# Attention inside a one-core transformer chain: a new table of order, one weighing block per group of heads, the input norm one sample ahead, and two alternating buffers

## The chip, the cores and the metric

The kernel runs on one NeuronCore of a Trainium2 chip. The metric is the device time of one execution in microseconds (us), as the median of several runs; lower is better.

## The reference

Four layers in a row on `x` of 8 samples x 512 tokens x 256 features. The change touches only the attention half of the first layer:

```python
x = _ln(src) * (1.0 + scale) + shift                 # norm of the input, modulated per sample
q = (x @ Wq + bq).reshape(B, S, N_HEAD, HEAD_DIM)    # 16 heads of 16; k and v likewise
scores = jnp.einsum('bhqd,bhkd->bhqk', q / math.sqrt(HEAD_DIM), k) + attention_bias
scores = jnp.where(src_mask, -jnp.inf, scores)
probs = jax.nn.softmax(scores, axis=-1)
ctx = jnp.einsum('bhqk,bhkd->bhqd', probs, v)        # merged to [B, S, D]
x = x + (ctx @ Wo + bo)                              # the residual is the scaled x, not src
```

Then follow a feed-forward part, an adapter layer, a pairwise rotation and a second adapter layer. `attention_bias` is 8 x 16 x 512 x 512 float32, 128 MiB, which is read once.

## The kernel before, in words

The attention part handles the samples b = 0 to 7 one after the other. A sample has 64 **steps** n, one for each head h = n // 4 and tile t = n % 4 of 128 queries. Each engine runs its own program over the steps, and semaphores join them. In step n:

- PE makes scores three steps ahead (`scores`, L581): 128 queries x 512 keys into one of three banks `s_bank`. For some tiles it adds the mask term by a second matmul (L583).
- DVE adds the bias two steps ahead and takes the row maximum (`add_bias`, L762), into one of four tiles `prob`.
- ACT takes the exponential in place (L937).
- PE transposes the 128 x 512 tile in four pieces (`turn`, L593) into one of two banks `t_bank`; ACT (L944) or DVE (L771, for the steps in `DVE_TAKES`) copies it to `pt`.
- After four heads, PE multiplies `pt` with the values for the whole group (`weigh(b, g, c)`, L607) for the four key blocks c. One float32 matmul stands as two records in the trace.

The mask is 0 or -1e30. For the tiles counted in `POOL_TILES[h]`, POOL adds it to the loaded bias in place (`mask_bias`, L1101, up to four tiles in one instruction), and the other tiles are the PE ones. The bias of one head is a load of 1 MiB into one of four buffers `big`; SP issues the load for head h + 4 when the last tile of head h has been read by `add_bias`.

Between the steps stand **spare uses** of two further banks, at the steps that the tables `TAIL`, `AHEAD`, `VALUES` and `GROUPS` give: `XT` transposes the normed x of the next sample, `Q`, `K`, `V` project it, `O` transposes a group's context, `C` and `W` are the output projection of the previous sample. POOL cuts the projections into three bf16 pieces (`cut`), SP stores the pieces to DRAM and loads them back stacked (`stack_q`, `stack_k`).

The norm of the next sample's x is made inside the same sample in which it is used: DVE takes the statistics at step 11, ACT takes the square root at step 12 (L949), DVE inverts it and norms four tiles at step 14 (`normalise`, L801), and PE transposes them at steps 14 and 15 (L629). The scaled result goes to `xt`. POOL copies it to `xres` (`keep_residual`, L1172), because `W` of that sample comes a whole sample later. POOL makes the mask term twice for each sample, once for heads 0 to 13 and once for heads 14 and 15 (L1078, L1087).

PE, ACT, POOL and SP run samples 1 to 6 in a hardware loop; DVE has its program written out.

## Time and profile before

| What | Value |
|---|---|
| Median of 3 runs | 1039.73 us (1037.82 to 1042.37) |
| Span of the profiled execution, first to last instruction | 1036.6 us |
| PE matmul busy | 956.1 us, 92% |
| DVE, ACT, POOL busy | 813.7, 734.7, 726.3 us |
| One of the six steady samples (290.70 to 374.66) | 83.96 us |
| Start and setup, up to the first `add_bias` | 39.8 us |
| All after 710 us (the end of attention, and the network part) | 326.6 us |

The profiled execution is described by its span; its own device time is not listed apart from it, and the median of the runs lies 3.1 us above the span. The busy shares are over the whole run. A steady sample is measured from the first `add_bias` of one sample to that of the next, so that its length is what a sample costs.

### The profile page before, as it was taken

What the parts mean: (1) busy time and instruction counts of PE and PEld (TensorE: products, weight loads), DVE (VectorE), ACT (ScalarE), POOL (GpSimd) and SP (SyncE); (2) the same over time, 40 slices, a digit from 0 to 9 for tenths busy, and PEclk for the clock granted to TensorE, in tenths of its full rate; (3) what the DMA queues carried; (4) which work ended last, traced back from release to release, by engine and by line L of the source; (5) the groups of instructions that cost most, each with busy time, mean ns of one, the idle gap of its engine ahead of it and who ended that gap; (6) DMA issues with size and microseconds to landing.
All of it is one profiled execution on the core that took longest, in us unless ns stands there. A gap on an engine that the chain in (4) does not pass through costs nothing. (4 is left out here: it accounts for less than half of the span.)

```text
span 1036.6 us, 20438 instructions
## 1 busy us (share of the span) xinstructions
PE 956.1 (92%) x5892; PEld 640.9 (62%) x5892; DVE 813.7 (78%) x2075; ACT 734.7 (71%) x1211; POOL 726.3 (70%) x596
## 2 busy tenths in 40 slices
PE   5879999999999999999999999898999999999963
PEld 4646556656655655755665665454777777777752
DVE  8887797878879879879787887874456877887697
ACT  3577887888798788788788878875446556655433
POOL 3487697788788878878778878777555567755631
PEclk9989999999999999999999999999999999999987
DMA  7978978997996997897799799752111111111001
GB/s 262 334 289 292 381 289 278 363 347 238 346 384 214 336 386 257 291 390 292 265 372 343 237 348 370 252 193 82 41 41 41 42 33 50 42 41 41 21 21 41
DMA packets 127535, 230.33 MB, mean 222 GB/s; under 512 B 5488, under 2 KB 53872, under 8 KB 123632
## 3 DMA queue, kind: packets, MB, share of 16 engines
q1 hardware_dynamic: 127472, 229.60, 62.0%
q8 instruction: 26, 0.43, 0.2%
q14 instruction: 37, 0.30, 0.1%
HBM read 187.63 MB, written 41.94 MB: 221 GB/s over the span
## 5 line engine op out<-in xcount | busy, mean ns | idle before, releaser
L937 ACT ACTIVATE prob<-prob,nmax 128x512 f32<-128x512 f32 x512 | 357.0, 729 | 59.6 <-DVE nmax L762 56.4
L762 DVE CUSTOM_DVE_ANT_0 prob<-s_bank,big 128x512 f32<-128x512 f32 x512 | 338.7, 684 | 69.7 <-POOL big L1101 40.3
L1101 POOL TENSOR_TENSOR big<-big,mterm_early 128x2048 f32<-128x2048 f32 (+2 forms) x88 | 305.3, 3484 | 71.5 <-DMA big<-in_fside_Bx16xSxS 62.3
L593 PEld LDWEIGHTS t_bank<-ident,prob 128*128 128x128 f32 x2048 | 238.1, 141 | 168.3 <-issue 51.5
L593 PE MATMUL t_bank<-ident,prob 128*128 128x128 f32 x2048 | 317.7, 278 | 15.9 <-ACT prob L937 6.7
L944 ACT COPY pt<-t_bank 128x512 f32<-128x512 f32 x312 | 181.1, 584 | 51.7 <-PE t_bank L593 50.6
L581 PE MATMUL s_bank<-stack_k,stack_q 128*128 128x512 bf16 x512 | 195.4, 382 | 1.3 <-DVE nmax L762 0.7
L771 DVE COPY pt<-t_bank 128x512 f32<-128x512 f32 x200 | 137.2, 686 | 34.9 <-PE t_bank L593 34.6
L2052 POOL TENSOR_TENSOR gl<-big,gh 128x512 fp32r<-128x512 f32 x64 | 84.6, 1329 | 69.8 <-DVE gh L1643 69.8
L607 PE MATMUL o_bank<-pt,val 128*32 128x512 f32 x1024 | 122.9, 598 | 1.2 <-ACT pt L944 0.7
L1905 ACT ACTIVATE big<-bank,late 128x512 f32<-128x512 f32 x62 | 42.7, 689 | 75.2 <-PE bank L1446 71.4
L1101 POOL TENSOR_TENSOR big<-big,mterm_late 128x1024 f32<-128x1024 f32 (+1 forms) x16 | 49.9, 3119 | 29.2 <-DMA big<-in_fside_Bx16xSxS 29.2
L581 PEld LDWEIGHTS s_bank<-stack_k,stack_q 128*128 128x128 bf16 x512 | 50.0, 98 | 25.4 <-DVE nmax L762 12.0
L607 PEld LDWEIGHTS o_bank<-pt,val 128*32 128x32 f32 x1024 | 26.9, 109 | 59.4 <-issue 55.7
L583 PE MATMUL s_bank<-mterm_early,ident_bf 128*128 128x512 bf16 x152 | 57.9, 381 | 0.0
L637 PE MATMUL spare<-xth,w_parts 128*128 128x512 f32 x128 | 52.6, 428 | 1.7 <-DVE xtl L809 1.7
L1464 PE MATMUL bank<-gh,w2h 128*128 128x512 f32 x128 | 53.5, 418 | 0.0
L1446 PE MATMUL bank<-xth,w1h 128*128 128x512 f32 x124 | 50.6, 408 | 1.0 <-PEq L291 1.0
L1464 PE MATMUL bank<-gh,w2l 128*128 128x512 f32 x128 | 50.5, 395 | 0.0
L1446 PE MATMUL bank<-xtl,w1h 128*128 128x512 f32 x124 | 49.0, 395 | 0.0
L1446 PE MATMUL bank<-xth,w1l 128*128 128x512 f32 x124 | 48.9, 395 | 0.0
L762 DVE DVE_READ_ACCUMULATOR2_ANT nmax<- 128x1 f32 x512 | 42.1, 82 | 0.0
(257 smaller groups left out, 1610.0 us busy)
## 6 DMA issues: line engine op xcount, KB each, us to landing
big<-in_fside_Bx16xSxS SPq DMA_DIRECT2D x128, 1024.0 KB, 8.0
pieces_dram<-pieces SPq DMA_DIRECT2D x64, 384.0 KB, 7.3
stack_q<-pieces_dram SPq DMA_DIRECT2D x15, 1024.0 KB, 8.3
stack_k<-pieces_dram SPq DMA_DIRECT2D x15, 1024.0 KB, 10.0
pieces_dram<-pieces SPq DMA_DIRECT2D x32, 256.0 KB, 7.6
xin<-in_x SPq DMA_DIRECT2D x8, 512.0 KB, 8.7
x_dram<-x SPq DMA_DIRECT2D x8, 512.0 KB, 2.6
x1r<-x_dram SPq DMA_DIRECT2D x8, 512.0 KB, 4.3
```

The costliest lines, as they stand in the source:

```text
L581: last = pe.matmul(bank, stack_q[:, h, t * P:(t + 1) * P], stack_k[:, h, :], start=True, stop=not by_pe)
L583: last = pe.matmul(bank, ident_bf[:], mterm[:, t, :], start=False, stop=True)
L593: last = pe.transpose(t_bank[n % 2][:, c * P:(c + 1) * P], prob[:, n % NT, c * P:(c + 1) * P], ident[:])
L607: last = pe.matmul(o_bank[VW * j:VW * (j + 1), :], val[:, c, G * g + j, :], pt[:, pt_slot(G * g + j), c, :], start=(c == 0), stop=(c == QT ...
L762: dve.tensor_tensor_reduce(out=prob[:, n % NT, :], in0=s_bank[n % 3][:, :], in1=bias[:, h % NB, t, :], scale=-1.0, scalar=3e38, op0=ALU.ad ...
L771: dve.tensor_copy(pt[:, pt_slot(h), :, t * P:(t + 1) * P], t_bank[n % 2][:, :].rearrange("p (c q) -> p c q", c=QT)).then_inc(evac[1].sem, 1)
L937: act.activation(tile, tile, ACT.Exp, bias=nmax[:, n % NT:n % NT + 1], scale=-1.0).then_inc(exped.sem, 1)
L944: act.copy(pt[:, pt_slot(h), :, t * P:(t + 1) * P], t_bank[n % 2][:, :].rearrange("p (c q) -> p c q", c=QT)).then_inc(evac[0].sem, 1)
L1101: pool.tensor_tensor(bias[:, h % NB, tiles], bias[:, h % NB, tiles], mterm[:, tiles], ALU.add).then_inc(masked.sem, 1)
L1446: last = pe.matmul(bank[f % 2][:, :], w[:, c, col], h[:, c, :], start=(n == 0), stop=(n == len(parts) - 1))
L1464: last = pe.matmul(bank[c][:, :], w[:, f, c * P:(c + 1) * P], gx[:, f, :], start=(m == 0), stop=(m == len(parts) - 1))
L2052: pool.tensor_tensor(gl[:, f], g[:, f % NGT], gh[:, f], ALU.subtract).then_inc(gl_done.sem, 1)
```

## The change

It does six things.

1. **One weighing block.** `weigh` for the four key blocks of a group stood as two blocks of two, two steps apart. Now all four stand together, at steps 18, 34, 50 and 2.
2. **The norm a sample ahead.** Statistics of the x of sample b + 1 are taken during sample b (steps 21, 26, 47, 48), aggregated at 49, and its four tiles are normed one by one at steps 57, 61, 62 and 63. The inverse root is a power of -0.5 on POOL (step 52), not a root on ACT. The load of x moves from the start of a sample to head 4 of the sample before. In the first sample, which has nobody ahead of it, this is squeezed into steps 3 to 11.
3. **Two buffers for the scaled x**, by parity of the sample; `xres` and `keep_residual` go.
4. **Two buffers for the mask term**, by parity; it is made once for each sample, and two PE waits become one.
5. **The table of order** is another: 46 instead of 43 tiles of a sample masked by POOL, 26 instead of 25 copies by DVE, all spare uses at other steps, and POOL's masks among its other work in another order.
6. **Written-out programs** for PE, ACT and POOL in place of their loops.

The core of the diff:

```diff
-POOL_TILES = (0, 4, 2, 4, 3, 4, 4, 2, 4, 4, 0, 0, 2, 4, 2, 4)
+POOL_TILES = (0, 4, 0, 4, 4, 4, 4, 4, 4, 4, 4, 3, 0, 4, 3, 0)
-HEADS_OF_LOADS = dict(x1=3, first=2, expert=4, W1=6, mask=5, store_0=7, store_1=11)
+HEADS_OF_LOADS = dict(x=4, x1=3, first=2, expert=4, W1=6, mask=5, store_0=6, store_1=13)
-TAIL = [("O", 3, 6, 1), ("C", 0, 7, 1), ("C", 1, 9, 1), ("W", 0, 10, 1), ("W", 1, 12, 1)]
+TAIL = [("O", 3, 4, 1), ("C", 0, 6, 1), ("C", 1, 8, 1), ("W", 0, 10, 1), ("W", 1, 13, 1)]
...
                     g, c = (n - WEIGH_AFTER) // 16, (n - WEIGH_AFTER) % 16
-                    if c in (0, 2) and (g >= 0 or not first):
-                        for part in (c, c + 1):
+                    if c == 0 and (g >= 0 or not first):
+                        for part in range(QT):
                             weigh(b if g >= 0 else b - 1, g % NG, part)
...
+            def normalise_tile(b, t):
+                if t == 0:
+                    dve.wait_ge(root_done.sem, root_done.at(b, 1))
+                done = dve.tensor_scalar(xin[:, t], xin[:, t], mv[:, t, 0:1], rstd[:, t:t + 1], ALU.subtract, ALU.mult)
+                if t == QT - 1:
+                    done.then_inc(xhat_done.sem, 1)
...
-                    dve.wait_ge(res_done.sem, res_done.at(b - back - 1, 1))
                     dve.wait_ge(x1_out.sem, x1_out.at(b - back, 0))
-                    dve.scalar_tensor_tensor(x1[:, i], s[:, :], vec["bo"][:, i:i + 1], xres[:, i],
+                    dve.scalar_tensor_tensor(x1[:, i], s[:, :], vec["bo"][:, i:i + 1], xts[(b - back) % 2][:, i],
                                              ALU.add, ALU.add).then_inc(x1_done.sem, 1)
...
+                    if ahead and n in STATISTICS_AT:
+                        statistics_of(b + 1, STATISTICS_AT.index(n))
+                    if ahead and n == AGGREGATE_AT:
+                        aggregate(b + 1)
+                    if ahead and n in NORMALISE_AT:
+                        normalise_tile(b + 1, NORMALISE_AT.index(n))
...
+            def inverse_root(b):
+                pool.wait_ge(shifted.sem, shifted.at(b, 1))
+                apart(pool, k["apart"])
+                pool.tensor_tensor(rstd[:], std[:], minus_half[:], ALU.pow).then_inc(root_done.sem, 1)
```

`statistics_of(b, t)` takes one tile; the one for t = 0 waits for the load of x. On SP, `load_x(b + 1)` waits until both halves of sample b's scaled x are made.

Three places show how instructions move. The first is PE around the first group's weighing in the first sample: scores (`s_bank`), transposes of a step (`t_bank`), and weighing (`o_bank`). Before:

```order
L581 MATMUL s_bank<-stack_k,stack_q 128x512
L607 MATMUL o_bank<-pt,val 32x512 x8
L593 MATMUL t_bank<-ident,prob 128x128 x4
L581 MATMUL s_bank<-stack_k,stack_q 128x512
L593 MATMUL t_bank<-ident,prob 128x128 x4
L581 MATMUL s_bank<-stack_k,stack_q 128x512
L607 MATMUL o_bank<-pt,val 32x512 x8
L593 MATMUL t_bank<-ident,prob 128x128 x4
```

And of the change:

```order
L622 MATMUL spare<-ident,xin 128x128 x4
L574 MATMUL s_bank<-stack_k,stack_q 128x512
L600 MATMUL o_bank<-pt,val 32x512 x16
L586 MATMUL t_bank<-ident,prob 128x128 x4
L574 MATMUL s_bank<-stack_k,stack_q 128x512
L586 MATMUL t_bank<-ident,prob 128x128 x4
```

The sixteen matmuls stand in one piece, and the second half of the transposed x stands right before them.

The second place is DVE behind the scaled x. In the change, the first statistics of the next sample (`stats<-xin`) come this soon after the second half of the scaled x (`xt_odd<-spare`), on which the load of `xin` waits:

```order
L833 TENSOR_SCALAR xt_odd<-spare,ada 128x512
L816 TENSOR_TENSOR xtl<-xt_odd,xth 128x512 x2
L755 ISA prob,nmax<-s_bank,big 128x512
L755 ISA nmax 128x1
L755 ISA prob,nmax<-s_bank,big 128x512
L755 ISA nmax 128x1
L764 COPY pt<-t_bank 128x4x128
L755 ISA prob,nmax<-s_bank,big 128x512
L755 ISA nmax 128x1
L764 COPY pt<-t_bank 128x4x128
L770 BN_STATS stats<-xin 128x6
```

Before, the four statistics stood together at step 11, with the load issued at the start of the sample:

```order
L762 ISA prob,nmax<-s_bank,big 128x512
L762 ISA nmax 128x1
L777 BN_STATS stats<-xin 128x6 x4
L780 BN_AGGR mv<-stats 128x2 x4
L762 ISA prob,nmax<-s_bank,big 128x512
```

So between the freed `xin` and its next use there are now three additions of bias and two copies, where there were eleven steps.

The third place is DVE at the end of a sample, where three of the four normed tiles now stand between the additions of bias:

```order
L755 ISA prob,nmax<-s_bank,big 128x512
L755 ISA nmax 128x1
L800 TENSOR_SCALAR xin<-xin,mv,rstd 128x256
L755 ISA prob,nmax<-s_bank,big 128x512
L755 ISA nmax 128x1
L800 TENSOR_SCALAR xin<-xin,mv,rstd 128x256
L755 ISA prob,nmax<-s_bank,big 128x512
L755 ISA nmax 128x1
L800 TENSOR_SCALAR xin<-xin,mv,rstd 128x256
L842 RECIPROCAL rsum<-spare 128x16
```

Before they stood together, right ahead of the transposes that read them:

```order
L799 RECIPROCAL rstd<-std 128x4
L801 TENSOR_SCALAR xin<-xin,mv,rstd 128x256 x4
L844 SCALAR_TENSOR_TENSOR x<-spare,vecs,xres 128x512
L762 ISA prob,nmax<-s_bank,big 128x512
L762 ISA nmax 128x1
```

They moved from step 14, where PE waits for them, to the last steps of the sample before.

## Rows read from the trace of the kernel before

**Rows 1.** The windows view: one steady sample (290.70 to 374.66), busy us by engine.

```profile
290.70:374.66 83.96, 80.98 (x559) 50.39 (x558) 69.67 (x184) 69.94 (x119) 67.76 (x54) 1.00 0.88 316
```

**Rows 2.** The groups of the whole run: line engine operation, busy, mean ns, idle before.

```profile
L937 ACT ACTIVATE prob<-prob,nmax 128x512 f32<-128x512 f32 x512 | 357.0, 729 | 59.6 <-DVE nmax L762 56.4
L762 DVE CUSTOM_DVE_ANT_0 prob<-s_bank,big 128x512 f32<-128x512 f32 x512 | 338.7, 684 | 69.7 <-POOL big L1101 40.3 <-PE s_bank L581 15.5 <-PE s_bank L583 7.4
...
L944 ACT COPY pt<-t_bank 128x512 f32<-128x512 f32 x312 | 181.1, 584 | 51.7 <-PE t_bank L593 50.6
L771 DVE COPY pt<-t_bank 128x512 f32<-128x512 f32 x200 | 137.2, 686 | 34.9 <-PE t_bank L593 34.6
L607 PE MATMUL o_bank<-pt,val 128*32 128x512 f32 x1024 | 122.9, 598 | 1.2 <-ACT pt L944 0.7 <-issue 0.5
...
L583 PE MATMUL s_bank<-mterm_early,ident_bf 128*128 128x512 bf16 x152 | 57.9, 381 | 0.0
```

**Rows 3.** The timeline of PE at the end of a group of weighing blocks: start, us.

```profile
317.05 0.38 PE L581 MATMUL s_bank<-stack_k,stack_q 128*128 128x512 bf16 x1
317.27 0.38 PE L583 MATMUL s_bank<-mterm_early,ident_bf 128*128 128x512 bf16 x1
317.48 0.60 PE L593 MATMUL t_bank<-ident,prob 128*128 128x128 f32 x4
317.92 0.38 PE L581 MATMUL s_bank<-stack_k,stack_q 128*128 128x512 bf16 x1
318.23 1.92 PE L607 MATMUL o_bank<-pt,val 128*32 128x512 f32 x16
320.08 0.66 PE L593 MATMUL t_bank<-ident,prob 128*128 128x128 f32 x4
```

**Rows 4.** The timeline of PE, 305.5 to 308.5: ahead of the output projection.

```profile
307.24 1.12 PE L662 MATMUL spare<-cont,wo 128*128 128x512 f32 x2 [0.76 <-ACT cont L976]
```

**Rows 5.** The timeline of PE, 312 to 316: ahead of the turned x.

```profile
313.41 0.66 PE L593 MATMUL t_bank<-ident,prob 128*128 128x128 f32 x4 [0.29 <-ACT prob L937]
315.47 0.66 PE L629 MATMUL spare<-ident,xin 128*128 128x128 f32 x4 [1.41 <-DVE xin L801]
```

**Rows 6.** The timeline of ACT in the same stretch.

```profile
309.65 1.28 ACT L949 ACT_TABLE_LOAD   x1
310.95 0.30 ACT L949 ACTIVATE std<-mv,eps 128x4 f32<-128x4 f32 x1
311.26 1.28 ACT L937 ACT_TABLE_LOAD   x1
```

**Rows 7.** The source view of L801, normalise: ns min/median/max.

```profile
L801 DVE TENSOR_SCALAR xin<-xin,mv,rstd x32: 398/774/4156, 13.7 to 566.6; 128x256 f32<-128x256 f32 x32
```

**Rows 8.** The timeline of POOL, one steady sample.

```profile
312.56 2.71 POOL L1087 TENSOR_SCALAR mterm_late<-mraw 128x512 bf16<-128x512 uint8 x4
316.25 1.05 POOL L1172 TENSOR_SCALAR xres<-xt 128x1024 f32<-128x1024 f32 x1 [0.98 <-issue]
...
326.16 4.12 POOL L1101 TENSOR_TENSOR big<-big,mterm_early 128x2048 f32<-128x2048 f32 x1 [2.69 <-DMA big<-in_fside_Bx16xSxS]
...
338.61 4.11 POOL L1101 TENSOR_TENSOR big<-big,mterm_early 128x2048 f32<-128x2048 f32 x1 [0.20 <-POOL pieces L1055]
...
377.44 4.09 POOL L1101 TENSOR_TENSOR big<-big,mterm_early 128x2048 f32<-128x2048 f32 x1 [3.28 <-DMA big<-in_fside_Bx16xSxS]
```

**Rows 9.** The timeline of the SP queue: a load of bias, and the first store of pieces.

```profile
320.39 0.38 SPq L430 DMA_DIRECT2D big<-in_fside_Bx16xSxS  x1
...
335.27 5.58 SPq L457 DMA_DIRECT2D pieces_dram<-pieces  x6
```

**Rows 10.** The DMA view: issues, KB each, us from issue to landing.

```profile
big<-in_fside_Bx16xSxS SPq DMA_DIRECT2D x128, 1024.0 KB, 8.0
...
xin<-in_x SPq DMA_DIRECT2D x8, 512.0 KB, 8.7
```

**Rows 11.** The timeline of PE in the first sample.

```profile
61.30 1.12 PE L629 MATMUL spare<-ident,xin 128*128 128x128 f32 x4 [3.39 <-DVE xin L801]
```

More of the change, by code:

```diff
@@ L268, in parts, with first_use @@
     return 2 if what in "QKVW" else 1
-def firsts(first, h, t):
-    return [t for n in range(QT * first, QT * h) if n % QT == t and t >= POOL_TILES[n // QT]]
+def first_use(h, t):
+    return all(t < tiles for tiles in POOL_TILES[:h])
 class SpareBanks:
@@ L737, in _ @@
             iteration(0, first=True)
-            with pe.Fori(1, B - 1) as b:
+            for b in range(1, B - 1):
                 iteration(b)
@@ L819, in spare_use @@
                 elif what == "XT":
-                    if i == 0 and not first:
-                        dve.wait_ge(res_done.sem, res_done.at(b - 1, 1))
                     if banks.kind == "last":
@@ L855, in iteration @@
                         take_turned(b, n - 1)
-                    if not last and n == STATISTICS_AT:
-                        statistics(b)
-                    if not last and n == NORMALISE_AT:
-                        normalise(b)
+                    if first and n == FIRST_STATISTICS_AT:
+                        for t in range(QT):
+                            statistics_of(b, t)
+                        aggregate(b)
+                    if first and n in FIRST_NORMALISE_AT:
+                        normalise_tile(b, FIRST_NORMALISE_AT.index(n))
+                    if ahead and n in STATISTICS_AT:
[4 more added lines that the diff above has]
+                        normalise_tile(b + 1, NORMALISE_AT.index(n))
                     if last and n == NORMALISE_LAST:
@@ L1026, in _ @@
             iteration(0, first=True)
-            with act.Fori(1, B - 1) as b:
+            for b in range(1, B - 1):
                 iteration(b)
@@ L1177, in iteration @@
                         copy_values(b - 1, NG - 1)
-                    if n == RESIDUAL_AT and not first:
-                        keep_residual(b - 1)
+                    if n == FIRST_ROOT_AT and first:
+                        inverse_root(b)
+                    if n == ROOT_AT and not last and not before_last:
+                        inverse_root(b + 1)
                     if not last and n in CUT_STEPS:
@@ L1207, in _ @@
             iteration(0, first=True)
-            before = links[0]
-            with pool.Fori(1, B - 1) as b:
+            for b in range(1, B - 2):
                 iteration(b)
-            assert links[0] - before == per_link
+            iteration(B - 2, before_last=True)
             iteration(B - 1, last=True)
```

219 lines of the change are left out of this document (99 added, 120 removed).

## The prediction

> **What bounds the kernel now.** I first cut the run into samples with the windows view. The steady ones are alike, so I read one: it takes 83.96 us, and PE is busy for 80.98 of them, DVE for 69.67, ACT for 69.94 and POOL for 67.76; the clock column stands at 1.00, PE's full level [rows 1]. The last column but one is the DMA share, 0.88. So PE ends the waits in the steady part, but no engine has more than 16.2 us to spare, and the DMA engines even less. Whatever shortens PE's chain by much more than 5 us per sample will meet the others.
>
> "Busy" hides how PE's time is made up, so I read starts, not durations. In the timeline a scores matmul is followed by the next instruction after 0.22 us, a mask matmul after 0.21 us, the four transposes of a step after 0.44 us [rows 3]. The 0.38 to 0.66 us of the rows are latencies that overlap. Then I looked for places where one start comes later than that: these are what the change can remove.
>
> **The weighing blocks.** Scores ahead of a weighing block hold PE for 0.31 us in place of 0.22, so going in costs 0.09 us. The block of 16 records takes 1.85 us until the next transposes begin. It is busy for 1.92 us, and one record lasts 0.60 on the mean [rows 2], so the last starts 1.32 us after the first: four rounds of four records at 0.44 us each are 1.76 us, which leaves 0.09 us for going out [rows 3]. That is about 0.2 us for each block. There are eight blocks in a sample and will be four: 0.8 us less. The page "TensorEngine Tiling (Array Packing)" of the Trainium skill says that changing the tiling mode drains the engine; the trace agrees, with the 0.09 us on either side.
>
> Longer blocks (3.7 us) starve the others only if these run out of work. PE is three steps of scores ahead, which is 2.1 us of DVE work (684 ns each) and 2.2 us of ACT work (729 ns each), and copies and spare evictions fill the rest [rows 2]. I cost this at nothing; without that cover it could be 1 us a block on DVE, which has the slack.
>
> **The mask matmuls.** Three fewer in a sample: 3 x 0.21 = 0.63 us less on PE [rows 3]. POOL pays: four tiles take 4.1 us, so three cost 3.1 us; it gets back 2.7 us for the second mask term and 1.05 us for the copy to `xres` [rows 8], and pays for the root of four columns. No row shows that root inside attention; it lies between nothing and a mask instruction of one tile (4.1 / 4 = 1.0 us), and I take the 1.0. POOL's total stays within 0.5 us of what it was (3.1 + 1.0 - 2.7 - 1.05). DVE takes one copy more (0.69 us) and ACT one less (0.58 us) [rows 2].
>
> **The output projection.** `W` stands right behind the second `C`, and waits 0.76 us for ACT's copy [rows 4]. In the new table a step lies between (8 and 10), which is at least 0.66 us of PE work plus its own transposes ahead of `W`. The wait goes: 0.76 us.
>
> **The norm.** ACT switches its table, takes a root of 0.30 us, and switches back: 2.86 us in which no exponential runs [rows 6]. Behind it PE waits 0.29 us for an exponential, and then 1.41 us for the normed tiles [rows 5]. With the norm a sample ahead both waits go: 1.70 us, and ACT has 2.9 us more room.
>
> **What replaces it.** Two new waits can arise, and I price both.
>
> First, x. The load of the next x can go out only when both halves of this sample's scaled x are made, at step 18, and DVE wants its first tile at step 21. A load of x lands 8.7 us after issue [rows 10]. What lies between on PE is one block of 3.7 us and two to four steps of 0.66 us, 5.0 to 6.3 us. So DVE waits 2.4 to 3.7 us in each sample. Behind it on DVE stand the additions of bias for steps 24 and later. PE has scores and exponentials for three steps in hand at that moment, and these steps are long because of the projections in them. Most of the wait is covered; between 0 and 3.7 us reach PE, and I take 0.6, near the covered end.
>
> Second, the port. A normed tile takes between 398 and 4156 ns, with a median of 774 [rows 7]. The 4.1 us are as long as one of POOL's mask instructions, 4.09 to 4.12 us [rows 8]: one instruction of DVE was held for one whole instruction of POOL. So far the tiles stood beside the four short instructions of the mask term (2.71 us together), hence the median. Now the last three stand at steps 61 to 63, while POOL's first mask of the next sample begins when its load lands: at 377.44, which is 2.8 us into the sample, before the change [rows 8]. One tile in each sample may meet it, and be held for between 0 and 4.1 us. PE then has two to three steps in hand again. Between 0 and 4.1 us I take 0.6, because only one of four can meet a given mask instruction and the next steps are PE's long ones.
>
> The rule for this is in "SBUF — State Buffer" of the Trainium skill (section "SBUF: two separate sides"): a VectorE instruction in its fast two-port mode and a GpSimd instruction exclude each other for the whole instruction. The trace agrees, by the 4156 ns.
>
> **The sum for a steady sample**: 0.80 + 0.63 + 0.76 + 1.70 = 3.89 us off, 1.2 us back, 2.7 us net, or 81.3 us in place of 84.0. DMA share becomes 0.88 x 84.0 / 81.3 = 0.91, still below one. Six such samples give 16.2 us.
>
> The first sample waits 3.39 us for its normed tiles alone [rows 11]; its statistics now come at step 3 and its tiles between POOL's first masks, each of which may hold one tile. I take 3 us off, between 0 and 7 (3.39 for the wait, 2.86 for the tables, 0.63 for the mask matmuls). The last sample loses switching, mask matmuls and the wait of `W`, but has no norm ahead: 0.8 + 0.63 + 0.76 = 2.2 us. Start and network part have the same work, apart from copies of nothing that PE waits for. Writing out the loops costs instruction fetches; DVE is written out already and is not short of instructions, so I cost it at zero.
>
> In all 16.2 + 3 + 2.2 = 21.4 us. Against the profiled span that is 1036.6 - 21.4 = 1015.2 us. The median of the runs lies 3.1 us above the span, so I say 1018 us.
>
> **Rivals.**
>
> A, *everything is gained* (0.18): neither new wait reaches PE. Then a steady sample gives 3.9 us, the first one 7, together 23.3 + 7 + 2.2 = 32.5, or 1007 us; ACT's extra room could add up to 1 us per sample, down to 1001. For it: PE's lead of three steps. Against: DVE's share on the last 16 steps, which get both the four tiles and the copies.
>
> B, *slower through the port* (0.13): the four tiles each meet a mask instruction and are held for half of it. That is 4 x 2.05 = 8.2 us per sample on DVE, and near the sample's end nothing covers it. The sample becomes 84.0 - 3.9 + 8.2 = 88.3 us, six of them cost 26 us more, and the time is about 1061 us. It decides from 1 us per tile on PE's path (3.9 / 4). For it: 4156 ns. Against: POOL still waits for its bias load 3.28 us at that point [rows 8], so it cannot be in mask instructions all the time.
>
> C, *given back* (0.12): the wait for x is not covered, 3.5 us of it reach PE, and the port costs 0.6. Then 3.9 - 4.1 is nothing for the steady samples, and the rest saves 2 to 5 us: 1035 to 1038 us.
>
> D, *the change's own POOL table comes late* (0.10). The load for head 11 now stands behind the first store of pieces in the SP queue, whose six issues hold the queue for 5.58 us [rows 9], and they wait for two cuts that POOL makes only behind head 8's mask. Head 11 was free of POOL before and now has three tiles on it. Counting 8.0 us to land [rows 10] after the last issue and 3.1 us of mask, its first tile is ready about when PE wants it, to within 1.5 us. If this and head 14 (now behind the last cut) come late, a sample loses 1.5 us more: 21.4 - 9 = 12.4 off, 1027 us. For it: DVE already waits 40.3 us in the run for POOL's masks [rows 2].
>
> **How the numbers follow.** My forecast (0.47) is 1018 us, with a range of its own of 1010 to 1026. The 80% range must reach A's middle and most of C: 1001 to 1037. Beyond lie B and a little of A. No change, within 0.5% (5.2 us, about what a measurement of this kernel can tell), is 1034.5 to 1045: C and the lower end of B, 0.12. Slower is the rest of B, 0.12. Faster is the forecast, A and D, and the edge of C: 0.76.
>
> **What would show it.** Steady samples of about 81 us; weighing in four blocks of 32 records with only four slow entries and exits; no table load on ACT inside attention; `W` without its wait; the transposes of xin without theirs. On DVE, a wait of the first BN_STATS for a DMA of 2.4 to 3.7 us, and normed tiles of 0.4 us with one of 1 to 4 us at the end of each sample. I am wrong if PE waits for DVE for more than 1.2 us behind those two places, or for POOL's masks of heads 9 to 14, or if DMA landing times rise above 9 us because the same bytes move in less time.

## The result, and the profile after

The changed kernel takes 1059.0 us (1053.2 to 1063.6, 4 runs) beside 1040.4 us for the kernel before: a ratio of 1.017, 95% interval 1.012 to 1.022. I forecast 1018 us. In all ratios below disturbed runs are left out, in the medians they are not, so where the two differ I go by the ratio. The kernel before took 1040.0 to 1041.3 us beside the other runs.

The profiled run of the change has a span of 1051.3 us, 14.7 us more than before. From first addition of bias to the next one, the samples take (us):

| Kernel | sample 0 | samples 1 to 6 | mean of 1 to 6 | sample 7 |
|---|---|---|---|---|
| before | 83.0 | 84.0 83.9 84.0 83.9 83.9 84.1 | 84.0 | 80.1 |
| changed | 90.1 | 85.3 83.3 82.9 86.3 90.4 80.6 | 84.8 | 82.9 |

So 7.1 us come in the first sample, 4.9 in the six steady ones, 2.8 in the last. The steady ones are not alike any more, which is the first thing to see. The windows view of the change, by sample (columns: stretch, us, busy us of PE, PEld, DVE, ACT, POOL, granted clock, DMA share, GB/s), then short stretches in the first and sixth sample:

```profile
38.80:128.80 90.00, 74.61 (x500) 48.99 (x499) 81.60 (x190) 65.04 (x109) 68.19 (x46) 0.92 0.87 309
214.20:297.40 83.20, 77.67 (x537) 49.69 (x538) 71.16 (x186) 66.53 (x113) 65.04 (x49) 0.98 0.89 310
466.60:557.00 90.40, 81.61 (x561) 53.05 (x559) 78.82 (x186) 67.74 (x114) 68.32 (x49) 0.96 0.86 299
...
56.00:60.00 4.00, 0.39 (x1) 0.10 (x1) 4.00 (x4) 0.72 (x1) 4.00 (x2) 0.57 0.51 190
60.00:64.00 4.00, 1.51 (x5) 0.85 (x5) 4.00 (x5) 0.72 (x1) 3.54 (x1) 0.50 0.00 0
64.00:68.00 4.00, 2.96 (x12) 2.47 (x13) 3.54 (x11) 3.08 (x6) 0.00 (x0) 0.50 0.21 66
498.00:502.00 4.00, 0.00 (x0) 0.00 (x0) 4.00 (x2) 0.00 (x0) 3.48 (x1) 0.79 0.59 242
502.00:506.00 4.00, 3.87 (x11) 2.56 (x11) 4.00 (x12) 2.55 (x4) 0.00 (x0) 0.50 0.07 10
```

Beside [rows 1], DVE is busy for 71 to 82 us instead of 70, though it has little more to do. In the stretches where PE stands, DVE and POOL are both busy all the time. And when PE starts again at 502, its clock is granted at 0.50, the lower level of 1.2 GHz.

The source view of the two lines that stretch (ns min/median/max, starts; the first answers to [rows 7]):

```profile
L800 DVE TENSOR_SCALAR xin<-xin,mv,rstd x28: 401/410/4118, 49.7 to 558.6; 128x256 f32<-128x256 f32 x28
L816 DVE TENSOR_TENSOR xtl<-xt,xth x10: 678/822/4621, 18.8 to 687.4; 128x512 fp32r<-128x512 f32 x10
L816 DVE TENSOR_TENSOR xtl<-xt_odd,xth x8: 678/2080/4527, 72.9 to 587.8; 128x512 fp32r<-128x512 f32 x8
```

Their timeline, with POOL's beside it, in the first sample and in the sixth (start, duration; x2 is the sum of two):

```profile
46.95 4.08 POOL L1103 TENSOR_TENSOR big<-big,mterm_even 128x2048 f32<-128x2048 f32 x1
51.33 12.21 POOL L1103 TENSOR_TENSOR big<-big,mterm_even 128x2048 f32<-128x2048 f32 x3 [0.29 <-DMA big<-in_fside_Bx16xSxS]
...
49.67 1.52 DVE L800 TENSOR_SCALAR xin<-xin,mv,rstd 128x256 f32<-128x256 f32 x1
52.32 3.23 DVE L800 TENSOR_SCALAR xin<-xin,mv,rstd 128x256 f32<-128x256 f32 x1
56.08 3.54 DVE L800 TENSOR_SCALAR xin<-xin,mv,rstd 128x256 f32<-128x256 f32 x1
60.75 2.94 DVE L800 TENSOR_SCALAR xin<-xin,mv,rstd 128x256 f32<-128x256 f32 x1
...
488.85 12.63 POOL L1103 TENSOR_TENSOR big<-big,mterm_odd 128x2048 f32<-128x2048 f32 x3 [0.74 <-DMA big<-in_fside_Bx16xSxS]
492.95 9.08 DVE L816 TENSOR_TENSOR xtl<-xt,xth 128x512 fp32r<-128x512 f32 x2
```

Each tile ends about 0.2 us after a mask instruction of POOL ends (the tiles at 51.2, 55.6, 59.6 and 63.7; the first mask at 51.0, the last at 63.5). I call "held" what a tile takes over its shortest time of 0.40 us, and a subtraction over 0.68 us. In samples 0 to 6 DVE is held for 54 us, 28 of them in the tiles, against 16 us before. What PE's other partners wait for, in the groups of the whole run (they answer to [rows 2]):

```profile
L953 ACT ACTIVATE prob<-prob,nmax 128x512 f32<-128x512 f32 x512 | 357.4, 722 | 88.9 <-DVE nmax L755 83.4
L586 PE MATMUL t_bank<-ident,prob 128*128 128x128 f32 x2048 | 318.9, 279 | 33.4 <-ACT prob L953 23.0
L574 PE MATMUL s_bank<-stack_k,stack_q 128*128 128x512 bf16 x512 | 198.1, 387 | 14.8 <-DVE nmax L755 14.3
L1080 POOL TENSOR_SCALAR val<-vst 128x64 f32<-128x64 f32 x128 | 28.5, 252 | 61.7 <-PE o_bank L600 50.6
```

The waits of PE for the normed tiles and for ACT's copy ahead of `W` are gone, as forecast. ACT's wait for the row maxima is 83.4 us where it was 56.4.

### The profile page after: what moved, and what is told of

Read it like the earlier page. It is cut to its first block and busy times, and to the rows that moved or that the text cites. A ratio compares the mean times of both kernels' runs of the same rounds, so it can differ in the third digit from the quotient of the medians.

```text
span 1051.3 us, 19070 instructions
## 1 busy us (share of the span) xinstructions
PE 947.9 (90%) x5868; PEld 654.1 (62%) x5868; DVE 849.7 (81%) x2084; ACT 718.0 (68%) x1182; POOL 729.4 (69%) x555
## 5 line engine op out<-in xcount | busy, mean ns | idle before, releaser
L953 ACT ACTIVATE prob<-prob,nmax 128x512 f32<-128x512 f32 x512 | 357.4, 722 | 88.9 <-DVE nmax L755 83.4
L755 DVE CUSTOM_DVE_ANT_0 prob<-s_bank,big 128x512 f32<-128x512 f32 x512 | 338.1, 684 | 34.5 <-POOL big L1103 14.6
L586 PEld LDWEIGHTS t_bank<-ident,prob 128*128 128x128 f32 x2048 | 247.3, 143 | 154.0 <-issue 66.5
L1103 POOL TENSOR_TENSOR big<-big,mterm_even 128x2048 f32<-128x2048 f32 (+1 forms) x48 | 189.9, 3970 | 36.8 <-DMA big<-in_fside_Bx16xSxS 27.8
L1103 POOL TENSOR_TENSOR big<-big,mterm_odd 128x2048 f32<-128x2048 f32 (+1 forms) x48 | 188.8, 3947 | 37.0 <-DMA big<-in_fside_Bx16xSxS 35.5
L960 ACT COPY pt<-t_bank 128x512 f32<-128x512 f32 x304 | 174.3, 575 | 22.1 <-PE t_bank L586 20.9
L764 DVE COPY pt<-t_bank 128x512 f32<-128x512 f32 x208 | 142.8, 686 | 46.8 <-PE t_bank L586 46.5
L600 PE MATMUL o_bank<-pt,val 128*32 128x512 f32 x1024 | 117.3, 599 | 0.2 <-ACT pt L960 0.2
L600 PEld LDWEIGHTS o_bank<-pt,val 128*32 128x32 f32 x1024 | 30.1, 110 | 68.5 <-issue 64.8
L1080 POOL TENSOR_SCALAR val<-vst 128x64 f32<-128x64 f32 x128 | 28.5, 252 | 61.7 <-PE o_bank L600 50.6
L630 PE MATMUL spare<-xth,w_parts 128*128 128x512 f32 x128 | 55.8, 444 | 11.0 <-issue 10.0
L1442 PE MATMUL bank<-xth,w1h 128*128 128x512 f32 x124 | 50.6, 408 | 1.0 <-PEq L289 1.0
L1460 PE MATMUL bank<-gh,w2l 128*128 128x512 f32 x128 | 50.6, 395 | 0.0
L983 ACT COPY osb<-o_bank 128x512 f32<-128x512 f32 x32 | 18.8, 586 | 38.3 <-PE o_bank L600 38.3
```

The source lines that it names most:

```text
L586: last = pe.transpose(t_bank[n % 2][:, c * P:(c + 1) * P], prob[:, n % NT, c * P:(c + 1) * P], ident[:])
L600: last = pe.matmul(o_bank[VW * j:VW * (j + 1), :], val[:, c, G * g + j, :], pt[:, pt_slot(G * g + j), c, :], start=(c == 0), stop=(c == QT ...
L630: last = pe.matmul(spare[n % 2][:, :], wx[name][:, part, i * P:(i + 1) * P], x[:, part, :], start=(part == m == 0), stop=(part == 1 and m ...
L755: dve.tensor_tensor_reduce(out=prob[:, n % NT, :], in0=s_bank[n % 3][:, :], in1=bias[:, h % NB, t, :], scale=-1.0, scalar=3e38, op0=ALU.ad ...
L764: dve.tensor_copy(pt[:, pt_slot(h), :, t * P:(t + 1) * P], t_bank[n % 2][:, :].rearrange("p (c q) -> p c q", c=QT)).then_inc(evac[1].sem, 1)
L953: act.activation(tile, tile, ACT.Exp, bias=nmax[:, n % NT:n % NT + 1], scale=-1.0).then_inc(exped.sem, 1)
```

## The experiments

Two theories at the start. **H**: DVE is held beside POOL's masks. **W** (not the spare use `W`): the single weighing block of 3.7 us leaves ACT and DVE without work, and they limit PE afterwards.

**1. Short mask instructions.** In the change, and in the kernel before:

```diff
-                tiles = slice(0, POOL_TILES[h])
-                pool.tensor_tensor(bias[:, h % NB, tiles], bias[:, h % NB, tiles], mterms[b % 2][:, tiles], ALU.add
-                                   ).then_inc(masked.sem, 1)
+                for t in range(POOL_TILES[h]):
+                    last = pool.tensor_tensor(bias[:, h % NB, t], bias[:, h % NB, t], mterms[b % 2][:, t], ALU.add)
+                last.then_inc(masked.sem, 1)
```

> The changed kernel, with POOL's mask additions one tile per instruction in place of up to four (1.0 us each in place of 4.1). Theory H (holding): the change is slower because DVE's normed tiles and its subtraction xtl, all of them between steps now full of POOL masks, are each held until POOL's instruction ends; over their shortest times they lose 53.7 us in the trace of after, 16.3 us before. With short instructions a hold ends after at most about 1.0 us; DVE loses under 25 us, and the time falls by 15 to 35 us, to 1025 to 1045. Theory T (table): POOL's masks come late through their order and through the copy of values that waits for the weighing; the time stays at 1059 within 5, or rises with POOL's extra instructions.

> The kernel before with the same split of the mask additions: the control. Theory H: there the holds cost 16.3 us on DVE, most of it covered, so between 0 and 5 us faster (1035 to 1041); if it gains as much as the split in the changed kernel, the holds are no cause of the difference. Theory T: the same or slower, as POOL has more instructions.

Change: 1055.8 us, ratio 1.012 (1.005 to 1.019). Before: 1040.9 us, ratio 1.001 (0.999 to 1.003). The profiled run of the first has a span of 1072.0 us, the longest of its four, so I read no total from it, but it shows why the edit brought little, if anything. Its source view:

```profile
L800 DVE TENSOR_SCALAR xin<-xin,mv,rstd x28: 398/634/1317, 50.0 to 566.1; 128x256 f32<-128x256 f32 x28
L816 DVE TENSOR_TENSOR xtl<-xt,xth x10: 678/1268/10109, 19.0 to 704.0; 128x512 fp32r<-128x512 f32 x10
L816 DVE TENSOR_TENSOR xtl<-xt_odd,xth x8: 679/1192/10472, 65.1 to 600.8; 128x512 fp32r<-128x512 f32 x8
```

And its timeline, POOL and DVE, late in the run:

```profile
579.00 21.28 POOL L1103 TENSOR_TENSOR big<-big,mterm_even 128x512 f32<-128x512 f32 x19
591.15 10.28 DVE L816 TENSOR_TENSOR xtl<-xt_odd,xth 128x512 fp32r<-128x512 f32 x2
```

A tile is held for one short instruction at most (1.3 us, where it was 4.1), and the first sample takes 84.3 us instead of 90.1: H is right there. The subtraction is held for the whole string: a mask of one tile takes 1.17 us, and DVE stands for 9.7 us, until the string of 19 ends at 600.3. So splitting moved the holding from the tiles to `xtl`. PE stands for that too: ahead of the projection `Q`, which reads `xtl`, it waits 33.6 us in five samples, up to 7.2 at a time. I had expected the holding to shrink for both.

**2. The first sample's norm late and in one piece.** All four tiles stand together at step 14:

```diff
-FIRST_STATISTICS_AT, FIRST_ROOT_AT, FIRST_NORMALISE_AT = 3, 5, (8, 9, 10, 11)
+FIRST_STATISTICS_AT, FIRST_ROOT_AT, FIRST_NORMALISE_AT = 11, 12, (14, 14, 14, 14)
```

> The changed kernel, with the norm of the first sample alone taken at the old steps (statistics 11, root 12, all four tiles together at 14) in place of 3, 5 and 8 to 11. The first sample is 7.1 us longer than before (90.05 against 82.97). Theory H: its four tiles stand next to POOL's first masks and three are held for 2.5 to 3.1 us (9.6 us in all); together at one step at most one is held, and the first sample comes back to 82 to 85 us, 5 to 7 us in the run. Theory T: the first sample stays near 90.

1056.5 us, ratio 1.014 (1.010 to 1.018): no better. The first sample takes 93.8 us in its profile, which is the longest of its four runs (span 1069.9 us). The tiles meet POOL's masks there as well (three are held, 10.0 us together), so the squeeze into steps 3 to 11 isn't the cause.

**3. The block, alone, and undone.** In the kernel before:

```diff
-                    if c in (0, 2) and (g >= 0 or not first):
-                        for part in (c, c + 1):
+                    if c == 0 and (g >= 0 or not first):
+                        for part in range(QT):
```

> The kernel before with one thing alone: the four key blocks of a group weighed in one piece, at the step where the first two stood. By my sum it gives 0.2 us for each of four blocks a sample, 6 us in all: 1034. If the longer block starves DVE or ACT, that gain is lost or turned round: 1040 or above.

1062.8 us, ratio 1.023 (1.020 to 1.026). This one edit makes the kernel at least as slow as the whole change does. All steady samples in its profile take 85.5 to 86.6 us, two more than before, and DVE is held for only 8 us in it, less than the 16 before: H has no part in it. Its timeline around a block, by engine:

```profile
347.73 3.64 PE L607 MATMUL o_bank<-pt,val 128*32 128x512 f32 x32
355.40 0.66 PE L593 MATMUL t_bank<-ident,prob 128*128 128x128 f32 x4 [0.62 <-DVE pt L771]
...
347.38 0.72 ACT L937 ACTIVATE prob<-prob,nmax 128x512 f32<-128x512 f32 x1
351.99 0.59 ACT L944 COPY pt<-t_bank 128x512 f32<-128x512 f32 x1 [3.89 <-PE t_bank L593]
354.77 0.72 ACT L937 ACTIVATE prob<-prob,nmax 128x512 f32<-128x512 f32 x1 [0.96 <-DVE nmax L762]
...
348.49 0.69 DVE L762 CUSTOM_DVE_ANT_0 prob<-s_bank,big 128x512 f32<-128x512 f32 x1
352.21 0.69 DVE L762 CUSTOM_DVE_ANT_0 prob<-s_bank,big 128x512 f32<-128x512 f32 x1 [3.02 <-PE s_bank L581]
```

ACT runs out of work 0.4 us into the block and stands 3.9 us; DVE stands 3.0. Then all three come back at once, and PE waits for their copies. PE's waits in four steady samples (206 to 542; us, times, longest), first this kernel's, then those of before:

```profile
PE t_bank L593 <- ACT pt L944: 5.6, 8, 1.2
PE t_bank L593 <- DVE pt L771: 3.9, 8, 0.6
PE spare L629 <- DVE xin L801: 3.7, 4, 1.1
```

```profile
PE spare L629 <- DVE xin L801: 5.2, 4, 1.4
PE spare L662 <- ACT cont L976: 3.0, 4, 0.8
PE t_bank L593 <- ACT prob L937: 1.2, 4, 0.3
```

The two rows for the copies are new: 9.5 us, 2.4 a sample. Then the reverse, in the change (spare uses of the sample before stand where they stood before, since the context is ready later), and a finer cut in the kernel before:

```diff
-WEIGH_AFTER = 18
-CONTEXT_AFTER = 19
+WEIGH_AFTER = 17
+CONTEXT_AFTER = 21
-TAIL = [("O", 3, 4, 1), ("C", 0, 6, 1), ("C", 1, 8, 1), ("W", 0, 10, 1), ("W", 1, 13, 1)]
+TAIL = [("O", 3, 6, 1), ("C", 0, 7, 1), ("C", 1, 9, 1), ("W", 0, 10, 1), ("W", 1, 13, 1)]
-                    if c == 0 and (g >= 0 or not first):
-                        for part in range(QT):
+                    if c in (0, 2) and (g >= 0 or not first):
+                        for part in (c, c + 1):
```

> The changed kernel with only its first part undone: weighing stands as two blocks of two key blocks again, at steps 17 and 19 of each group's sixteen instead of one block at 18; the context is taken at 21, and the context transpose and first output projections of the sample before stand at 6, 7 and 9 as before. Everything else is the change's. Theory W (the single block of four starves PE afterwards, because ACT and DVE have nothing to do during it and then limit PE): the block alone cost 22 us in the kernel before, so this gives back 15 to 25 us: 1034 to 1044 us, and a steady sample of 82 to 83 us. Theory H (the holding of DVE beside POOL's masks, 53.7 us over the run against 16.3, is the cost): the time stays at 1053 to 1060 us. If the whole sum of the prediction was right but for the block (its 0.8 us per sample taken away): about 1023 us.

1050.4 us, ratio 1.010 (1.007 to 1.014): 8.6 us back, about half of what W alone had to bring. So the block is a cause, and not the only one. That it costs 2.3% in the kernel before and 0.7% here, where the steps around it are others, no run explains.

```diff
-                    if c in (0, 2) and (g >= 0 or not first):
-                        for part in (c, c + 1):
+                    if c < QT and (g >= 0 or not first):
+                        for part in (c,):
```

> The kernel before with the weighing split further: four blocks of one key block each, at steps 17, 18, 19 and 20, in place of two blocks of two at 17 and 19. The same 64 matmuls per group. Theory W (what counts is how long PE leaves the score and turning banks alone: 1.8 us a block now, 0.95 then): the same time or up to 5 us faster, 1035 to 1040 us. Rival S (each switch into and out of the weighing shape costs 0.2 us of PE, as the prediction took it, and 8 more switches per sample are paid in full): +1.6 us a sample or so, 1048 to 1053 us.

1048.3 us, ratio 1.008 (1.005 to 1.010), with steady samples of 85.0 us, 1.0 more than before. Eight more blocks a sample cost 1.0 us, so a switch costs about 0.13 us net. Switching does cost, though less than my 0.2 us, and two blocks of two are the best of the three cuts: four are slower by the switches, one by the starving.

**4. Written-out programs.** PE's alone, then PE's, ACT's and POOL's:

```diff
-            with pe.Fori(1, B - 1) as b:
+            for b in range(1, B - 1):
```

> The kernel before with only PE's loop over samples 1 to 6 written out, so that PE fetches about seven times the program. Rival F (part of what the change lost is the fetch of a written-out program): 1043 us or more, and PE idle time put down to issue rises by several us. The prediction, which cost it at nothing: 1037 to 1042 us.

> The kernel before with the loops over samples 1 to 6 of PE, ACT and POOL all written out (part 6 of the change by itself; DVE's is written out already, SP's stays a loop). With PE's alone written out the median was 1043.9 against 1040.7, hardly more than the measurement can tell. Rival F (the fetch of written-out programs costs): another 1 to 4 us, 1044 to 1048 us. The prediction, which cost it at nothing: 1038 to 1042 us, and then the 3 us of PE's alone were scatter.

1043.9 us, ratio 1.002 (1.000 to 1.005), and 1041.6 us, ratio 1.002 (1.000 to 1.004). At the edge of what can be told: about 2 us, at most 5.

**5. The norm on ACT.** The change with two blocks, and the tiles on ACT:

```diff
-                done = dve.tensor_scalar(xin[:, t], xin[:, t], mv[:, t, 0:1], rstd[:, t:t + 1], ALU.subtract, ALU.mult)
+                    dve.scalar_tensor_tensor(nshift[:], mv[:, :, 0], -1.0, rstd[:], ALU.mult, ALU.mult
+                                             ).then_inc(norm_ready.sem, 1)
...
+                    act.wait_ge(norm_ready.sem, norm_ready.at(b, 1))
+                done = act.activation(xin[:, t], xin[:, t], ACT.Identity, bias=nshift[:, t:t + 1], scale=rstd[:, t:t + 1])
```

> The changed kernel with two weighing blocks (as in the run before, 1050.4 us), and with the four normed tiles of each sample, the first included, made by ACT (x times rstd plus a shift that one small DVE instruction makes) at the same steps in place of DVE. Theory H (DVE is held by the port that it shares with POOL's mask additions, in every tile of the norm and in the low part of x): the hold of the normed tiles, 27.5 us in the changed kernel, 9.6 of them in the first sample, is gone; the first sample comes back from 88.8 to about 84 us, the steady ones by 0.5 to 1.5 us: 1038 to 1046 us. Rival N (the first sample is long for another reason, the norm's chain itself or the masks' order): the first sample stays at 87 us or more, and the time at 1047 to 1052 us.

1039.8 us, ratio 0.998 (0.996 to 1.000). The first sample takes 83.9 us instead of 88.8, as H said. The same with `xtl` by POOL, behind its mask of step 18:

```diff
-                    dve.tensor_tensor(xtl[:, c], xts[(b + 1) % 2][:, c], xth[:, c], ALU.subtract).then_inc(xtl_done.sem, 1)
+                    pool.wait_ge(xth_done.sem, xth_done.at(b, c + 1))
+                    pool.tensor_tensor(xtl[:, c], xts[(b + 1) % 2][:, c], xth[:, c], ALU.subtract).then_inc(xtl_done.sem, 1)
```

> As the run before, and the subtraction that makes xtl done by POOL, behind its mask of step 18, in place of DVE. Theory H: DVE is held by nothing any more, so that its hold over the shortest times goes from about 20 to about 5 us. If the place on POOL costs nothing, 1035 to 1043 us. Against it: POOL stands in the wait for the scaled x while masks of the next heads are due, so Q at step 20 comes later and the masks of steps 20 and 21 too; if that costs 1 us or more a sample, the time is no better than with DVE, 1043 to 1050 us.

1081.4 us, ratio 1.039 (1.036 to 1.042): a miss. DVE is held for 2 us in all there, but POOL now stands in queue order before `xth` (27.0 us in four samples), and its masks come late: PE waits 23.0 us for exponentials. An engine with masks behind it is no place for an instruction that waits. Then the fourth corner, the change with its one block and only the edit of the norm tiles:

> The changed kernel, with its one weighing block, and only the four normed tiles moved from DVE to ACT: the fourth corner beside the change (1059.0), the change with two blocks (1050.4) and that with two blocks and the norm on ACT (1039.8). If the two losses are apart and add up: 1059.0 - 10.7 = 1048.3, within 1045 to 1052 us. If the single block costs as much here as alone in the kernel before (22 us) and the two cover each other in the change, 1056 to 1062 us. If the holding is all of it and the block costs nothing without it, 1038 to 1042 us.

1049.8 us, ratio 1.005 (1.002 to 1.009). The four corners, as ratio to the kernel before:

| | norm tiles on DVE | on ACT |
|---|---|---|
| one block | 1.017 (the change) | 1.005 |
| two blocks | 1.010 | 0.998 |

The block costs 0.7% in either column, the tiles on DVE 1.2% in either row (0.9 and 1.0% by the medians); each ratio is known to about 0.4%. The kernel of the fourth corner scatters most, from 1036.9 to 1065.3 us. So within the measurement the two edits add up, and are together 1.9%: all of the loss. Two things they don't settle. The tiles on ACT also take 0.40 us each, 11 us in the run, off DVE's own work, which the steady samples do not tell from the holding; in the first sample the split masks do, with the tiles still on DVE and 84.3 us.

The other is how the block costs. `Q` reads what the subtraction writes, and PE starts it 0.1 us after the subtraction ends; the profile puts this wait down to issue. Here is `Q` in the sixth sample of the change, then PE's wait at that place (39 to 720; us, times, longest) in the change, with two blocks, with one block and the tiles on ACT, and with both edits:

```profile
502.13 0.76 PE L630 MATMUL spare<-xth,w_parts 128*128 128x512 f32 x1 [5.15 <-issue]
...
PE spare L630 <- issue: 10.0, 5, 5.2
PE spare L630 <- issue: 0.4, 2, 0.3
PE spare L632 <- issue: 12.5, 7, 5.1
PE spare L632 <- issue: 2.7, 2, 2.3
```

With one block PE waits about 10 us longer for the subtraction, which is held for 26 and 31 us in samples 0 to 6, with two blocks for 12 and 14. PE's other waits are 46 and 36 us with one block, 47 and 32 with two. So by these waits the block's cost under the new table lies mainly in the held subtraction, and not, as in the kernel before, in partners that run out of work: the two causes are apart as edits, but both go through DVE's being held beside POOL's masks. This is read from the traces; no run has the one block without that holding.

**6. Where the expected gain went.** With both out, the kernel is only as fast as before. So I put the old table under parts 2, 3, 4 and 6, with two blocks; the norm once on ACT, once on DVE:

```diff
-POOL_TILES = (0, 4, 0, 4, 4, 4, 4, 4, 4, 4, 4, 3, 0, 4, 3, 0)
+POOL_TILES = (0, 4, 2, 4, 3, 4, 4, 2, 4, 4, 0, 0, 2, 4, 2, 4)
-MASK_AT = (-2, 5, 17, 18, 20, 20, 21, 25, 26, 27, 30, 45)
+MASK_AT = (-6, 1, 3, 7, 10, 15, 19, 20, 25, 46, 48, 49, 54)
... and the spare uses, value copies, DVE_TAKES, HIGH_STEP and LOW_STEP of before
```

> The run with the norm on ACT and two weighing blocks (1039.8 us), with the table of order of the kernel before as well: tiles masked by POOL and the places of its masks, DVE's copies, and all spare uses, value copies, and the steps of the high and low parts. What is left of the change are the norm a sample ahead (on ACT), the two buffers of the scaled x and of the mask term, and the written-out programs. Theory G (the prediction's gain of the norm ahead is real, PE 1.70 us and 0.76 of the output projection a sample, and the new table gives it back by its own waits): 1024 to 1034 us, a steady sample of 81.5 to 83. Rival Z (there is no such gain, because PE's wait for the norm was slack that is waited for elsewhere): 1037 to 1043 us, a steady sample of about 84.

> The same with the normed tiles on DVE, as the change has them, at steps 57, 61, 62 and 63 (8 to 11 in the first sample). So it is the run with two weighing blocks (1050.4 us) with the table of before. Theory H (beside POOL's masks each normed tile holds DVE for up to 4 us; POOL's masks of the next sample stand at 58, with the mask term at 54): 6 to 12 us above the run with ACT; the first sample 87 us or more. If the holding came from the new table's places alone, the two agree within 3 us.

1042.6 us, ratio 1.001 (0.999 to 1.003), and 1060.7 us, ratio 1.018 (1.013 to 1.022). The second is H once more, and dearer: the tiles are held for 23 us there, for 24 in the run with two blocks alone, but cost 1.7% instead of 1.2. In the first, DVE's waits (206 to 542) hold the row that I had forecast for the change, and that the change itself has only once in these samples, with 1.1 us:

```profile
DVE prob L757 <- PE s_bank L576: 28.0, 20, 2.0
DVE stats L772 <- DMA xin<-in_x: 10.2, 4, 2.8
```

Is it the landing of the bias that keeps the gain? I loaded only two of the four tiles of each head's bias; half of the bias is left out of the computation, and the other tiles keep what was there. In the kernel before, and in the one with both losses out:

```diff
-                sp.dma_start(bias[:, h % NB], bias_flat[:, bass.ds(b * H + h, 1)].rearrange("p o t k -> p (o t) k")
+                sp.dma_start(bias[:, h % NB, 0:2], bias_flat[:, bass.ds(b * H + h, 1), 0:2].rearrange("p o t k -> p (o t) k")
```

> The kernel before with only tiles 0 and 1 of each head's bias loaded (512 KB instead of 1 MiB), so that the other two tiles hold what was there: half of the bias is left out of the computation, all instructions of the engines stay. Theory D (the landing of bias sets the pace of a sample, DMA share 0.88, so that what PE waits for less elsewhere it waits for at the bias): 5 us faster or more, under 1036 us, and POOL's 100 us or so of waits for landings mostly gone. Theory C (the chain of scores, bias, exponential and turning between the engines sets it): 1037 to 1042 us, with POOL's waits moved to other releasers.

> The change with two blocks and the norm on ACT (1039.8 us) with the same half of the bias left out. Theory D: the expected gain of the norm ahead, about 2.5 us a sample, shows once the landing is out of the way, so this is 10 to 16 us faster than the kernel before with half the bias, near 1022 us. Theory C: it is within 4 us of that kernel.

1072.5 us, ratio 1.027 (1.022 to 1.032), and 1068.8 us, ratio 1.026 (1.023 to 1.029). For the first both theories missed: with 65 MB less of 230 to move it is slower by some 30 us. The second is so too, and lies within 4 us of the first, which is all that theory C had said of it. The subtraction in the first of them (source view), and PE's wait for it (206 to 542):

```profile
L809 DVE TENSOR_TENSOR xtl<-xt,xth x18: 684/1432/4981, 18.6 to 699.7; 128x512 fp32r<-128x512 f32 x18
```

```profile
PE spare L637 <- DVE xtl L809: 13.5, 4, 3.4
```

In the kernel before, the longest subtraction takes 1.4 us. POOL's masks start when the bias lands; landing earlier (3.4 us after issue instead of 8.0), they meet the subtraction in each steady sample, and PE waits 3.4 us for it. In the 4 us behind such a wait (245 to 249) the granted clock is 0.50; a steady sample is 4.8 us longer than before. The holding is a matter of phase, not of the change's tiles alone.

Two ends remained. In the kernel with two blocks and the norm on ACT, the tiles three steps later, and a mask ahead of the copy of values at which POOL waited (50.6 us in the groups above):

```diff
-AGGREGATE_AT, ROOT_AT, NORMALISE_AT = (21, 26, 47, 48), 49, 52, (57, 61, 62, 63)
+AGGREGATE_AT, ROOT_AT, NORMALISE_AT = (21, 26, 47, 48), 49, 52, (60, 61, 62, 63)
```

> The change with two blocks and the norm on ACT, with the first normed tile at step 60 instead of 57 (60, 61, 62, 63). In the run with 57, POOL makes the inverse root at 282.4 us of a sample in which step 57 comes at about 281, so that ACT stands before it with copies and exponentials behind it, and PE waits 0.25 and 0.62 us for the copies at 281.6 and 283.1. Theory C: these 0.9 us a sample come back, and the time is 1034 to 1038 us. If they are taken up by the next wait: 1038 to 1041 us.

```diff
-MASK_AT = (-2, 5, 17, 18, 20, 20, 21, 25, 26, 27, 30, 45)
+MASK_AT = (-2, 4, 17, 18, 20, 20, 21, 25, 26, 27, 30, 45)
```

> The change with two blocks and the norm on ACT (1039.8 us), with one number of the table changed: POOL's mask of step 5 at step 4, so that it stands before the copy of the last group's values and not behind it. In that run POOL waits 28.3 us in four samples (up to 7.7 at a time) at this copy for the last weighing block, with three masks standing behind it, which then run in a string up to the place of the xtl subtraction. If the wait costs: POOL's wait at the copy falls to 4 us a sample or less, the string is shorter, and the time is 1034 to 1038 us. If POOL's reserve covers it, 1038 to 1042 us. If the mask now holds DVE at another place, more.

1051.3 us (1042.6 to 1058.3), ratio 1.011 (1.005 to 1.018), and 1037.5 us, ratio 0.999 (0.996 to 1.001). The first is slower, with the widest scatter, and I have no shown cause: its profile is its fastest run, and has one sample of 88.4 us, in which PE waits 4.1 us for a row maximum and a subtraction takes 2.9 us. In the second POOL's wait is gone, and it brings nothing beyond the measurement. Last, the statistics later, under the old table:

```diff
-AGGREGATE_AT, ROOT_AT, NORMALISE_AT = (21, 26, 47, 48), 49, 52, (57, 61, 62, 63)
+AGGREGATE_AT, ROOT_AT, NORMALISE_AT = (26, 28, 47, 48), 49, 52, (57, 61, 62, 63)
```

> The run with the norm a sample ahead on ACT and the table of before (1042.6 us), with the first two tiles of the statistics at steps 26 and 28 instead of 21 and 26. In that run the wait that the prediction named appears: DVE stands 2.11 us before the first statistics for the landing of x, and PE 1.14 us for the exponential behind it. If these come back: 6 samples x 1.1 = 7 us, 1034 to 1038 us, faster than the kernel before. If PE's time goes to the next wait of the chain, as it did with the norm itself: 1039 to 1043 us.

**1031.1 us (1029.5 to 1031.6), ratio 0.992 (0.989 to 0.995): faster than both kernels.** Its window of a steady sample, and PE's waits in four:

```profile
200.10:283.50 83.40, 81.02 (x559) 50.63 (x559) 66.83 (x182) 69.36 (x120) 65.30 (x51) 1.00 0.91 320
```

```profile
PE t_bank L588 <- ACT pt L961: 5.2, 16, 0.5
PE spare L657 <- ACT cont L1000: 2.5, 4, 0.6
PE t_bank L588 <- ACT prob L954: 0.7, 4, 0.2
```

The first sample takes 78.1 us (83.0 before), a steady one 83.3 (84.0). So the wait for x, where it stands, costs 0.9%, some 10 us (1042.6 to 1031.1; the two ran beside the kernel before at 1041.3 and 1040.6). PE's wait of 5.2 us for the normed tiles is gone, and 5.2 us for ACT's copies stand in its place: ACT has the four tiles now, 2.5 us a sample, and these waits stand right behind them (at 202.3, 203.9, 280.1 and 282.3 in the window's sample). This is where most of the norm's steady gain goes.

## Why the prediction was wrong, step by step

- **The step that failed first**: "Longer blocks (3.7 us) starve the others only if these run out of work. … I cost this at nothing". They do run out: with the block alone in the kernel before, ACT does 0.4 us into the block, and the kernel loses 2.3%. I had counted three steps of scores as 2.1 us of work in hand; but DVE is two steps ahead and ACT one, so that at the block's start most of that work is done, and four key blocks last longer than what is left. In the change the block costs 0.7%, 7 us, where I had 6 us of gain (0.8 us in each sample). There PE's added wait is the one ahead of `Q` for the held subtraction, 10.0 us against 0.4, so the starving is shown for the kernel before only, and the other term that I had at nothing, `xtl` below, carries most of it by PE's waits.
- **Switching**, 0.2 us a block: right in kind, 0.13 us net in the run with four blocks.
- **The port** was mis-sized. I took 0.6 us a sample of the tiles reaching PE, and they cost 1.2%, 12 us in all. My bound of 4.1 us for one tile was right, and so was "One tile in each sample may meet it" for the six steady samples, where one is held for 2.4 to 3.7 us. Wrong was the first sample: I took 3 us off it, and all four tiles were held, 9.6 us together; with the tiles on ACT it is 4.9 and 7.4 us shorter. What is left of the 12 us is, by my estimate, about 1 us a steady sample instead of 0.6. Rival B had this mechanism and 1061 us, but all four tiles in every sample; only the first had that.
- **Not priced at all: the subtraction of `xtl`**, held for up to 4.6 us each, 26 us in samples 0 to 6, in front of `Q`, where PE waits 10.0 us for it. The section of the Trainium skill that I cited ("SBUF — State Buffer", "SBUF: two separate sides") names a VectorE instruction with two SBUF inputs beside the fast mode, and I took only the latter from it. The trace agrees: the subtraction has two such inputs and is held, 4.6 us beside masks of 4.1. The run with split masks goes beyond that section's "for the whole instruction": there it was held for a whole string of them, up to 10.5 us, and the measurement decides.
- **The wait for x** did not appear in the change (1.1 us once): its load lands in 6.3 us there instead of 8.7. With the old table it did, 2.6 us on the mean on DVE, as forecast, and cost 0.9%, some 10 us, where I had 0.6 in each of six samples.
- **The norm's 1.70 us and `W`'s 0.76**: the waits are gone, as put. But PE waits for ACT and DVE nearby instead. In the fastest kernel a steady sample is 0.7 us shorter, and the first 4.9 us, where I had 3; the old table in it brings the wait of `W` back (2.5 us in four samples).
- **Mask matmuls, POOL's table (D), loops**: Rival D did not show; DVE's wait for masks fell from 40.3 to 14.6 us. The loops may cost 2 us. What the three matmuls bring by themselves was not tried, nor the old table's other differences one by one.
- **The sum** was made against PE alone, as if what is cut from one of its waits shortened the sample. It does so only if ACT and DVE are ahead at that place.

The loss is thus the block and the tiles, each shown by an edit and its reverse or by two rows of the table. That the block acts through `xtl` in the change is read from PE's waits. What the change would take without that holding stays open: under the new table the only kernel without it had a new wait on POOL.

## What to carry to other kernels

When an engine does one long piece that feeds nobody, count the work its partners have *left* at that moment, from the timeline, and not the depth of their buffers; in the kernel before, the time lost in the piece was not caught up (2 us a sample). Before moving a VectorE instruction, look whether the trace has its form held: here the normed tiles (SBUF to SBUF) and the subtraction (two SBUF inputs) were. Then keep it away from long GpSimd instructions, or give it to ScalarE; splitting the GpSimd instruction need not help. And after a win, look for a wait that has moved behind it, also one that the profile books as issue: here two numbers of the table turned 1042.6 into 1031.1 us.

## What the runs showed of the hardware that I had not expected

- A string of back-to-back GpSimd instructions of 1.17 us held the subtraction (two SBUF inputs) for 9.7 to 10.5 us, to the end of the string, while a normed tile (one SBUF input) got in after one of them, at 1.3 us at most.
- 28% less to move made the kernel before 2.7% slower: POOL's instructions came to lie beside DVE's subtraction, which took 4.6 us in each steady sample instead of 1.4 at most.
- In the change a stand of PE costs more than itself: after 498 to 502 with no matmul the granted clock is 0.50 in the next 4 us (four transposes take 1.09 us at 504.00, and 0.60 at 490.17), and in the first sample it is 0.57, 0.50 and 0.50 in the three stretches from 56 to 68, where the kernel before has 0.83, 0.50 and 0.82.
